# Attention of 16 batches on one core: value operands of 96 and 64 columns, and one copy out of the value banks

## The reference, cut to what matters

```
def _L0_cond_ref(x, mask, Wq, Wo):      # x (16, 512, 1024), mask (16, 1024), 8 heads of 64
    q = xt @ Wq.T                       # xt: x with its last two axes swapped
    qh = q.reshape(B, T, NH, dk).transpose(0, 2, 1, 3)
    scores = scale * jnp.einsum('bhqd,bhkd->bhqk', qh, qh)
    logits = (scores * cmask + (1.0 - cmask) * NEG) * rmask
    attn = jax.nn.softmax(logits, axis=-1)
    ctx = jnp.einsum('bhqk,bhkd->bhqd', attn, qh)
    out = ctx.transpose(0, 2, 1, 3).reshape(B, T, D) @ Wo.T
    return jnp.transpose(out, (0, 2, 1))
x = x + _L0_cond_ref(x, cond_2048, Wq, Wo)
x = x + _L1_cond_ref(x, cond_2048[:, None, :], L1_cond_b)   # causal depthwise convolution, 16 taps
```

## Time and profile before

| | before |
|---|---|
| runs, us | 4293.75, 4297.24, 4297.84 (median 4297.24) |
| profiled execution | span 4288.0 us from first to last instruction; the median of the timed runs is 9.2 us above it |
| PE busy | 4140.9 us (97%) |
| ACT busy | 2849.5 us (66%) |
| POOL, DVE busy | 2602.8 us (61%), 2495.8 us (58%) |
| DMA | 16 engines busy a third of the time, 385 MB |

### The profile page before, as it was taken

One profiled execution on the slowest core, in us unless ns is written; L12 is line 12 of the kernel. 1 busy time (PEld: TensorE's weight loads), 2 busy tenths in 40 slices (PEclk: granted clock), 3 DMA queues, 4 the chain that ended last, 5 costly groups with the idle time before them and its releaser, 6 DMA issues. The chain is left out here.

```text
span 4288.0 us, 56952 instructions
## 1 busy us (share of the span) xinstructions
PE 4140.9 (97%) x18688; PEld 2978.4 (69%) x18688; DVE 2495.8 (58%) x2260; ACT 2849.5 (66%) x3905; POOL 2602.8 (61%) x1044
## 2 busy tenths in 40 slices
PE   7999999999999999999999999999999999999799
PEld 4776767677676767767676776767677676767598
DVE  4664555556455655645565565556556565655676
ACT  4775767667576766757676675767667576766465
POOL 4775757667576766757676675757667575766300
PEclk8999999999999999999999999999999999999999
DMA  3323333232333323233333323333332333332488
GB/s 103 82 67 71 80 83 94 69 89 65 72 80 81 94 71 87 65 74 80 79 94 73 85 65 76 79 77 94 75 84 67 77 79 75 94 74 60 128 283 269
DMA packets 286191, 385.34 MB, mean 90 GB/s; under 512 B 148947, under 2 KB 217171, under 8 KB 285782
## 3 DMA queue, kind: packets, MB, share of 16 engines
q1 hardware_dynamic: 285910, 381.57, 34.9%
HBM read 112.28 MB, written 67.11 MB: 42 GB/s over the span
## 5 line engine op out<-in xcount | busy, mean ns | idle before, releaser
L698 POOL TENSOR_TENSOR plo<-p,phi 128x1024 fp32r<-128x1024 f32 x1024 | 2597.5, 2548 | 1405.1 <-ACT phi L628 1390.2
L742 DVE TENSOR_REDUCE mrow<-misc 128x1 f32<-128x1024 f32 x1024 | 1215.0, 1218 | 1076.9 <-PE misc L470 1073.2
L626 ACT ACTIVATE p<-sc 128x512 f32<-128x512 f32 x2048 | 1109.9, 594 | 848.7 <-PE sc L509 622.6
L522 PE MATMUL pv<-phi,val 128*128 128x512 f32 x4096 | 1136.1, 399 | 42.2 <-issue 42.2
L628 ACT ACTIVATE phi<-p 128x1024 fp32r<-128x1024 f32 x1024 | 1086.6, 1061 | 32.5
L522 PEld LDWEIGHTS pv<-phi,val 128*128 128x128 f32 x4096 | 766.5, 188 | 252.1 <-issue 76.6
L508 PE MATMUL sc<-quer,keys 128*128 128x512 f32 x2048 | 916.8, 448 | 22.9 <-issue 17.5
L509 PE MATMUL sc<-quer,keys 96*128 96x512 f32 x2048 | 810.1, 396 | 0.0
L526 PE MATMUL pv<-plo,val 128*128 128x512 f32 x2048 | 648.3, 397 | 0.7 <-POOL plo L698 0.7
L470 PE MATMUL misc<-quer,keys 128*128 128x512 f32 x2048 | 599.9, 401 | 23.4 <-DMA keys<-lo 11.7
L508 PEld LDWEIGHTS sc<-quer,keys 128*128 128x128 f32 x2048 | 386.3, 189 | 199.9 <-issue 75.0
(11 more groups left out here) (67 smaller groups left out, 2646.8 us busy)
## 6 DMA issues: line engine op xcount, KB each, us to landing
keys<-hi SPq DMA_DIRECT2D x256, 256.0 KB, 3.1
quer<-mhi SPq DMA_DIRECT2D x256, 256.0 KB, 4.4
keys<-lo SPq DMA_DIRECT2D x128, 256.0 KB, 4.9
quer<-mlo SPq DMA_DIRECT2D x128, 256.0 KB, 3.8
xo<-x SPq DMA_DIRECT2D x64, 512.0 KB, 3.9
x<-xo SPq DMA_DIRECT2D x64, 512.0 KB, 5.0
xin<-x SPq DMA_DIRECT2D x16, 2048.0 KB, 13.4
out<-stage SPq DMA_DIRECT2D x64, 512.0 KB, 6.4
```

The source lines that it names most:

```text
L522: pe.matmul(pv[:, half(h)], val[:, i, t, part, :], phi[:, t % NPHI, half(h)], start=(t == 0 and part == 0), stop=False)
L626: act.activation(p32[:, t % NP32, half(h)], sc[:, h, :], ACT.Exp, scale=SCALE).then_inc(s_p32, 1)
L698: pool.tensor_tensor(plo[:, t % NPLO, :], p32[:, t % NP32, :], phi[:, t % NPHI, :].bitcast(F32), ALU.subtract).then_inc(s_plo, 1)
L742: reduced = dve.tensor_reduce(mrow[:, q:q + 1], misc[:, k, :], AX.X, ALU.max)
```

## The change

`val` gets 96 columns for each operand: 64 values first, then 32 ones (high operand). The low operand is used with its 64 values alone. So the context always lands on partitions 0 to 63 of `pv` and the sums on 64 to 95, whatever i is. One ACT copy of 96 partitions moves `pv` to a new tile `pvs` and signals `s_cab`. SP then spreads the rows: one DMA of 64 partitions to `ca` and two of 32 to `den`, with a new semaphore `s_ctx`; DVE's reciprocals wait for it, and so does ACT's next copy. For the very last head there is no DMA: ACT copies straight from `pv`, in two halves of 512 columns with three copies each.

```
@@ context, PE
                 for h in range(2):
-                    for part in range(2):
-                        pe.matmul(pv[:, half(h)], val[:, i, t, part, :], phi[:, t % NPHI, half(h)],
-                                  start=(t == 0 and part == 0), stop=False)
+                    pe.matmul(pv[0:VC, half(h)], val[:, i, t, 0, :], phi[:, t % NPHI, half(h)],
+                              start=(t == 0), stop=False)
+                    pe.matmul(pv[0:DK, half(h)], val[:, i, t, 1, 0:DK], phi[:, t % NPHI, half(h)],
+                              start=False, stop=False)
                 pe.wait_ge(s_plo, n + 1)
                 for h in range(2):
-                    last = pe.matmul(pv[:, half(h)], val[:, i, t, 0, :], plo[:, t % NPLO, half(h)],
+                    last = pe.matmul(pv[0:VC, half(h)], val[:, i, t, 0, :], plo[:, t % NPLO, half(h)],
                                      start=False, stop=(t == KT - 1))
@@ copy_context, ACT
                 act.wait_ge(s_pv, (head(b, p, i) + 1) * KT)
+                if not (isinstance(b, int) and b == 0 and p == 0 and i == 0):
+                    act.wait_ge(s_ctx, CTX * head(b, p, i))
                 if i == 0 and not (isinstance(b, int) and b == 0 and p < 2):
                     act.wait_ge(s_cnorm, pair(b, p) - 1)
-                mine, other = slice(DK * i, DK * i + DK), slice(DK - DK * i, P - DK * i)
-                act.activation(ca[mine, p % 2, :], pv[mine, :], ACT.Copy)
-                act.activation(den[mine, p % 2, :], pv[other, :], ACT.Copy).then_inc(s_cab, 1)
+                act.activation(pvs[:], pv[0:VC, :], ACT.Copy).then_inc(s_cab, 1)
@@ SP
+            def context_rows(b, p, i):
+                sp.wait_ge(s_cab, head(b, p, i) + 1)
+                at = DK * i
+                sp.dma_start(ca[at:at + DK, p % 2, :], pvs[0:DK, :]).then_inc(s_ctx, 16)
+                for r in range(DK // ONES):
+                    sp.dma_start(den[at + r * ONES:at + (r + 1) * ONES, p % 2, :], pvs[DK:VC, :]).then_inc(s_ctx, 16)
...
                             operands2(nb, np_, ni, None if first else head(b, p, i) * KT * 2)
+                        if not (phase == "first" and p == 0 and i == 0):
+                            context_rows(*head_before(b, p, i))
                         if phase != "first" and (p, i) == (0, 1):
                             load_xo(b - 1, 0, True)
                             load_xo(b - 1, 1, True)
@@ reciprocals, DVE
                 if part == 0:
-                    dve.wait_ge(s_cab, head(b, p, 1) + 1)
+                    dve.wait_ge(s_ctx, CTX * (head(b, p, 1) + 1))
@@ the end of the attention, ACT
-                copy_context(B - 1, PAIRS - 1, 1)
+                for h in range(2):
+                    last_context(h)
```

More of the change, by code:

```diff
@@ L23 @@
 BAND = 96
+ONES = 32
+VC = DK + ONES
 NP32, NPHI, NPLO = 2, 4, 4
@@ L212, in build_attention @@
         keys, quer, keys2, quer2 = pre.keys, pre.quer, pre.keys2, pre.quer2
-        val = sb("val", [P, 2, KT, 2, P], F32R)
+        val = sb("val", [P, 2, KT, 2, VC], F32R)
         mrow = sb("mrow", [P, KT], F32)
@@ L217, in build_attention @@
         p32, phi, plo = pre.p32, pre.phi, pre.plo
+        pvs = sb("pvs", [VC, T], F32)
         ca = sb("ca", [P, 2, T], F32)
@@ L253, in build_attention @@
         s_cab = sem("s_cab")
+        s_ctx = sem("s_ctx")
         s_rden = sem("s_rden")
@@ L265, in pair @@
             return b * PAIRS + p
+        CTX = 16 * (1 + DK // ONES)
         def bank(phase, b, step, item):
@@ L545, in start @@
                 pe.wait_ge(s_ident, 3)
-                pe.wait_ge(s_ones, 4)
+                pe.wait_ge(s_ones, 2)
                 do("start", 0, 0, "head", PHASES["start"]["head"], (0, 0, 0))
@@ L601, in values @@
                     act.wait_ge(s_pv, (head(*nxt) - 1) * KT)
-                at = DK * nxt[2]
-                act.activation(val[:, nxt[2], :, :, at:at + DK],
+                act.activation(val[:, nxt[2], :, :, 0:DK],
                                misc[:, k, :].rearrange("p (k c d) -> p k c d", c=2, d=DK), ACT.Copy).then_inc(s_val, 1)
@@ L610, in copy_context, with last_context @@
                 act.wait_ge(s_pv, (head(b, p, i) + 1) * KT)
+                if not (isinstance(b, int) and b == 0 and p == 0 and i == 0):
+                    act.wait_ge(s_ctx, CTX * head(b, p, i))
                 if i == 0 and not (isinstance(b, int) and b == 0 and p < 2):
                     act.wait_ge(s_cnorm, pair(b, p) - 1)
-                mine, other = slice(DK * i, DK * i + DK), slice(DK - DK * i, P - DK * i)
-                act.activation(ca[mine, p % 2, :], pv[mine, :], ACT.Copy)
-                act.activation(den[mine, p % 2, :], pv[other, :], ACT.Copy).then_inc(s_cab, 1)
+                act.activation(pvs[:], pv[0:VC, :], ACT.Copy).then_inc(s_cab, 1)
+            def last_context(h):
+                if h == 0:
+                    act.wait_ge(s_pv, KT * NH * B)
+                at, p = DK, (PAIRS - 1) % 2
+                act.activation(ca[at:P, p, half(h)], pv[0:DK, half(h)], ACT.Copy)
+                for r in range(DK // ONES):
+                    done = act.activation(den[at + r * ONES:at + (r + 1) * ONES, p, half(h)], pv[DK:VC, half(h)], ACT.Copy)
+                done.then_inc(s_cab, 1)
             def exponentials(b, p, i, t, first):
@@ L667, in constants @@
                 for i in range(2):
-                    fill = slice(DK - DK * i, P - DK * i)
-                    pool.memset(val[:, i, :, 0, fill].bitcast(F32), 1.0).then_inc(s_ones, 1)
-                    pool.memset(val[:, i, :, 1, fill].bitcast(F32), 0.0).then_inc(s_ones, 1)
+                    pool.memset(val[:, i, :, 0, DK:VC].bitcast(F32), 1.0).then_inc(s_ones, 1)
             def masks():
@@ L769, in reciprocals, with last_reciprocals @@
                 if part == 0:
-                    dve.wait_ge(s_cab, head(b, p, 1) + 1)
+                    dve.wait_ge(s_ctx, CTX * (head(b, p, 1) + 1))
                 d = den[:, p % 2, tok(part)]
+                dve.reciprocal(d, d).then_inc(s_rden, 1)
+            def last_reciprocals(part):
+                d = den[:, (PAIRS - 1) % 2, tok(part)]
                 dve.reciprocal(d, d).then_inc(s_rden, 1)
@@ L860, in end @@
                 for h, done in enumerate((s_half, s_cnorm)):
+                    dve.wait_ge(s_cab, NH * B + h)
+                    if h == 0:
+                        dve.wait_ge(s_ctx, CTX * (NH * B - 1))
                     for part in range(h * KT // 2, (h + 1) * KT // 2):
-                        reciprocals(B - 1, p, part)
+                        last_reciprocals(part)
                     dve.wait_ge(s_rden, KT * pair(B - 1, p) + (h + 1) * KT // 2)
```

## The result

| | before | changed |
|---|---|---|
| median of the runs, us | 4297.11 | 4340.24 (4339.64 to 4348.5) |
| ratio | | 1.0109, 95% interval 1.0096 to 1.0121: 1.1% slower |
| span of the profiled execution | 4288.0 | 4338.1 |
| mean granted clock | 0.994 | 0.982 |

The two spans are 50.1 us apart, the medians 43.1: the profiled execution of the kernel before was a quick one. The 27 timed runs of that kernel beside the experiments have spans of 4291.1 to 4301.7 us, at a mean clock of 0.991 to 0.994. So differences against the kernel before that are read from the two traces can be some 7 us too large.

The account below looks back on a forecast made before the run. PE, busy for 97% of the span, was taken to bound the kernel. Span 4288.0 - 46 (copy) + 95 (late `xo`) + 32 (clock) = 4369 us, plus 9.2 for the median: 4378 us, range 4255 to 4440.

Parts of the forecast that it names:

- The copy: Ahead of the value product at t = 2, i = 1: PE's 0.95 us wait for the second ACT copy goes, -46 us.
- The late block of `xo`: Pair 1, i = 1: SP's wait for the copy delays store and load of `xo`, stopping PE at t = 4; +95 us.
- 6.3 us per batch: Delay of `out` 7 in pair 1, i = 1 from late `xo`, in each of fifteen batches: +95 us.
- The lower bound: Least delay from late `xo`, with a 5.0 us store and three issues of 0.42: 4.4 us per batch, +66 us.
- The clock: After PE's stop in pair 1, i = 1 the clock falls to half pace: 2.1 us per batch, +32 us.
- The case without it: Rival: PE's stop at t = 4 is there but its clock stays up; 4346 us, chance 0.28.
- The pace: Value product's matmuls stay 0.235 us apart despite narrower loaded operands: 0 us.
- The row of 8 columns: Maxima transpose with an 8-column operand, whose load left the pace at 0.235 us; taken as evidence for 0 us.
- The 9.2 us: Added to the forecast span because the runs' median lay 9.2 us above the span before.
- Drains by changes of width: Rival: each change of operand width in the value product empties the array, +672 us, 5050 us; chance 0.06.
- Streaming at the bf16 pace: Rival: narrow operands speed the value product's matmuls by 18 ns, -111 us, 4267 us; chance 0.13.
- A hidden block: Rival: the late `xo` block in pair 1, i = 1 costs nothing; 4251 us, chance 0.06.

Follow-up runs that it names:

- the wait alone: Kernel before, plus only a wait for the value-bank copy (carried by a 32-byte DMA) ahead of the `xo` store in pair 1, i = 1: 4388.49 us.
- full width: Like rows behind xo, but all value operands 128 columns wide, one 64-row DMA for the sums and a copy of 128 partitions: 4250.05 us.
- low operand of 96 columns: Like rows behind xo, but the low operand padded with 32 columns of zeros, so widths 96 and 64 never alternate: 4240.7 us.
- rows between store and load: Like rows behind xo, but in pair 1, i = 1 the three context moves stand between the `xo` store and its load: 4242.33 us.
- rows behind xo: Changed kernel, but in each head SP issues the three context moves after the store and load of `xo`, not ahead of them: 4236.93 us.

## Why the prediction was right, point by point

The forecast was 4378 us, with a range of 4255 to 4440. The measured 4340.24 lies well inside, but the range is wide enough to hold no change at all, and the loss is 43 us where 81 were forecast. What speaks for the prediction are its signs: PE's waits with the cause "issue" fell from 50 places to one, DVE waits for `xo` in 16 places in place of one (9.5 us in each of the 15 new ones, where 8 to 9 were said), PE stops twice in each of 15 batches, the clock falls, and the value product keeps its pace within 2 ns.

- **The copy.** Forecast -46 us. The steps t = 2 of i = 1 give 47.1 us, and the second copy put back costs 48 us. Shown. (With a copy of 1.061 us the gain would still be the whole 0.95 us by the forecast's own times, 1945.09 against 1945.13, and not the 0.91 that it states.)
- **The late block of `xo`.** Forecast: the store goes out 12.9 us into the head, the load 19.5 us, the block is added from 23.4 us, and two stops of PE follow in banks A and B. Measured: 13.3, 18.9 and 22.2 us, and the stops in that order. The mechanism is shown from both sides: the order undone takes it away, the wait alone brings it into the kernel before. The term "6.3 us per batch" was too large: 11.36 - 6.29 = 5.07 us, 76 us in all and not 95. Two durations were at fault. From issue of the store to issue of the load it was 5.55 us and not 6.6, with as many bytes just ahead of it. The transfers ahead were further along, though, as batch 7 shows: in the kernel before, the last of them landed 3.4 us behind the issue of the store, in the changed one 2.2 us, and with the wait alone, where only 32 bytes stand ahead, the store landed after 4.8 us (6.5 before, 5.4 changed). That fits a store that takes longer the more is still under way at its issue; no run varies this alone. And the block was there about 3.35 us after the issue of its load, where the median of all 64 loads said 3.9; the loads at this place take a median of 3.5 us (3.4 to 3.8) in the kernel before too, so the row of the place would have been the better one. A third duration was off the other way: from the end of the copy to the store it took 2.06 us and not 1.7. The lower bound was added up wrong as well: a store of 5.0 us and issues of 0.42 take 2.04 us off 6.3, which leaves 4.2 us per batch and not 4.4, 63 us and not 66; the measured 5.07 lies above either.
- **The clock.** Forecast: it falls, 2.1 us per batch. It does: 13.04 - 11.36 = 1.7 us, 25 us in all and not 32. The case without it (4346 us) is closer to the measured time than my main figure of 4378, but by its mechanism it is wrong, and its closeness is luck: the errors of the other terms just add up that way.
- **The pace.** Forecast 0 us. It is -2 ns a matmul, -12 us (full width). The row of 8 columns was too coarse to show it; that its matmul streams "in two passes" no run shows, only that it took 0.105 us for 128 columns. The steps other than the two named are only 3.8 us shorter in the changed kernel, and the distances show where the other 8 us are. The first steps of the batches are 6.0 us longer in all: in three batches the clock fell there (7.94 to 7.97 us and not about 6.4), and the first step of the program took 9.54 us and not 7.97. The last steps ahead of the loop's turn are 2.2 us longer. All others are 12.0 us shorter. In the kernel before the clock fell at no turn, but that is the one quick execution; whether the change makes such falls more frequent stays open.
- **The sum.** -47 + 76 + 25 - 4 = +50 us, which is the difference of the spans (the -4 is what is left over). The forecast of 4369 us for the span is 31 us over 4338.1: 19 from the late block, 7 from the clock, 4 from the rest, 1 from the copy. The 9.2 us that I added for the median were a chance of one execution: this time the median lies 2.1 us above the span, and a timed run is 1.7 to 1.8 us above its own span. That is the other 7 us of the 38 by which 4378 is too high.
- **The rivals.** Drains by changes of width: none. The Trainium skill (TensorEngine Tiling (Array Packing), Key Properties) asks for a drain when the tiling mode changes; if the 64-column operands were such a change, four switches a step would show, and neither the distances (1.389 us for six matmuls, where 128 columns take 1.400) nor the low operand of 96 columns show one. Streaming at the bf16 pace: 2 ns of the 18. A hidden block: no, but the rows between store and load show how near it was: a load 6.4 us later than before costs almost nothing (13.25 us into the head and not 6.83), one 12.0 us later (18.87) costs 5 us per batch.

## What to carry to other kernels

A wait that is put into an in-order DMA queue is paid by what stands behind it, however little its own DMAs cost: here three moves that nobody hurried for held up a store, the load behind the store, an addition, a bank, and so PE. Put new waits behind the transfers with the nearest deadline, and count the whole chain to the next wait of the bounding engine. A stop of the bounding engine can also cost its clock: here that made a loss of 76 us a third larger. And compare a second trace with the first only after you know how far executions of one kernel lie apart; here it was some 7 us, as much as the smallest terms.

## What the runs showed of the hardware that was not expected

- ACT's copy of 1024 columns out of the banks takes 1.014 to 1.019 us for 32, 64, 96 and 128 partitions, so one wide copy in place of two narrow ones halves the time.
- The time of a weight load goes with its columns: 188 ns for 128, 162 for 96, 135 for 64, that is 0.83 ns a column. The Trainium skill (TensorE: Matmul & The Clock Gate, LDWEIGHTS) gives a load the number of columns over 1.2, in ns; the slope agrees, while a record is some 81 ns longer than that. The matmuls behind it gain only 2 ns of it.
- A stop of 2.9 to 3.5 us, one maxima product, and a second stop of 1.1 to 1.6 us were enough for the clock to fall to 1.2 GHz in each of the 15 batches. With the first stop filled but for 1.0 us at most it still fell in 10 of 15, with both filled (0.7 us at most left open) it stood in all of them. And a shorter hole can do it: with rows behind xo the clock fell at the start of two batches of the 16, behind the hole that the loop's turn leaves there. It fell so in three batches of the changed kernel, in five with the low operand of 96 columns, and in none of the profiled execution of the kernel before. One of the two in the timeline and the windows of rows behind xo:

```profile
2482.28 0.50 PE L524 MATMUL sc<-quer,keys 128*128 128x512 f32 x1 [1.97 <-issue]
```

```profile
2483.20:2486.60 3.40, 3.40 (x11) 2.26 (x10) 2.32 (x2) 1.87 (x3) 1.03 (x1) 0.56 0.01 2
```

The holes overlap: in rows behind xo the clock fell behind the holes of 1.97 and 1.70 us, and stood behind one of 1.96 us (the profile's idle time of PE). I had taken holes of 0.95 us as harmless and weighed longer ones by how near they come to 6.37; some of less than 2 us cost the clock too, and the length of the hole alone does not tell which.
